# Four edits at the seams between the stages of a graph network stack

## The chip, the cores and the metric

The kernel runs on one core of a Trainium2 chip. A core has TensorE (PE, matrix products), VectorE (DVE), ScalarE (ACT), GpSimd (POOL) and SyncE (SP, which here issues every DMA). The metric is the device time of one execution in microseconds, smaller is better. Weight loads of TensorE are shown apart, as PEld.

## The reference

128 graphs of 128 nodes with 128 features go through four layers, each followed by a residual sum and a layer norm:

```python
x = _layernorm(x + _L0_gnn_ref(x, adj, ...))   # prelu(adj @ (x W) + bias)
x = _layernorm(x + _L1_gnn_ref(x, adj, ...))   # adj @ (x W) + bias
x = _layernorm(x + _L2_gnn_ref(x, adj, nodemask, ...))
x = _layernorm(x + _L3_gnn_ref(x, adj, ...))

# _L2_gnn_ref: five gated steps over the same adjacency
A = (adj != 0).astype(x.dtype)
h = x
for l in range(5):
    m = jnp.einsum('bnd,de->bne', h, weight[l])
    agg = jnp.einsum('bij,bid->bjd', A, m)
    h = _gru_cell(agg, h, w_ih, w_hh, b_ih, b_hh)
return h * mask[..., None]

# _L3_gnn_ref: five node groups (25, 9, 7, 6 and 6 of the first 25 nodes), two graph convolutions each
h = _graph_conv(x_g, adj_g, W1[g], b1[g])      # relu(norm_adj @ (x W1) + b1), 256 hidden features
out_g = _graph_conv(h, adj_g, W2[g], b2[g])
fused = fused.at[:, idx, :].add(norm_w[g] * out_g)
```

## The kernel before

The kernel has three stages, and each engine has one program that goes through them in order; engines meet only at semaphores.

**Stage A** computes the first two layers, four graphs in a step, 32 steps (`STEPS_A`). A step is spread over six pipeline slots (`has(0)` to `has(5)`, a lag of 0 to 5 behind the newest step), so each engine runs `step_a` 37 times; the last five are a tail in which fewer and fewer slots have work. The slot of lag 3 forms the products of the second layer from `X1` (PE L1269, the last products being those with `yT`), lag 5 is ScalarE writing the normed result `x2` (L774, four instructions), after GpSimd has made its shift and scale (`NM1`, L621 and L625). `run_a` takes a function that is to be called ahead of one step of the tail: ScalarE copies the first two items' `x2` into the high halves of `X_OF` ahead of step 32 (L781), and VectorE makes the low halves (L1074) and the 0/1 adjacencies `A16` (L1078) ahead of step 34. All of VectorE's normalization (L915 statistics, L919 aggregation, L926 the normed `X1`) is in the same program.

**Stage B** is the gated layer. An item is four graphs at one of the five gated steps; there are 4 streams, 8 rounds, 160 items. A slot of `slot_b` serves several items at different lags: an item's products are at lag 2, its ScalarE work at lags 2 and 3, its last VectorE work at lag 4. For one item TensorE does, in order: three passes for `R` from the turned state `HT_HI`/`HT_LO` (L1313, L1314, L1318), eight small products with `A16` (L1342, bank `P_B`), three passes for `Z` and three for `N`, then nine passes with `PT_HI` and `PT_LO`. ScalarE writes `PT_HI` (L792) and VectorE `PT_LO` (L1143) from `P_B`; ScalarE applies the sigmoids (L822 for R, L849 for Z) and the tanh (L799). State is turned by DMA transpositions which SP issues: L532 for a gated step above the first, L529 for the first gated step of a stream in a round (its source is `X_OF`), L548 for the result. SP also issues the adjacency loads `load_b` (L490), and after the item with number 20 (`TURN`, the last of round 0) the weights of stage C, `v1` and `v2`, in two DMAs (L497, L499). GpSimd waits for all of `x2` before stage B, then makes `HT` for the first gated steps (L659), the low halves (L635), and late in a stream the sums and masks `YB` (L651, L640, L667).

**Stage C** is the last layer on 16 graphs a step, eight steps (`step_c`), with the norm of all nodes beside it. The first one begins with `support(0)` on TensorE (L1307), which is issued in the last slot of stage B; ScalarE copies it out of PSUM as `SP_T` (L868), TensorE multiplies by `v1` (`hid`, L1386) into two hidden halves, ScalarE and VectorE apply the bias and the relu (L889, L1214), and `v2` follows (L1419). VectorE adds the groups (L1179, seven instructions) and TensorE turns the sums (L1398). On ScalarE the copy of `support(0)` stands behind the end of `slot_b`, whose last work is the high half of the last item's state (L816), and that waits for the state itself (`b_h`, VectorE L1124). Steps of stage C run the leftovers of stage B in `rest(k)`.

## Time and profile before

| | |
|---|---|
| time, median of 3 runs | 1030.77 us (1025.63 to 1034.74) |
| the profiled execution, its own time | 1028.89 us |
| its span | 1027.1 us |
| busy share of PE, DVE, ACT, POOL | 94%, 84%, 79%, 78% |
| mean granted clock of TensorE | 0.979 |
| chain of work that ended last | PE 74%, DVE 17%, issue 3%, POOL 2%, ACT 1%, DMA 1%, SPq 1% |

The busy shares tell which engine has least idle time over the whole, not what each stage waits for. The chain is followed back from the last instruction: its shares say who set the end. A granted clock of 1.00 is TensorE's 2.4 GHz, 0.50 is 1.2 GHz. The span is 1.8 us shorter than the execution's own time.

### The profile page before, as it was taken

What the parts mean: (1) busy time and instruction counts of PE and PEld (TensorE: products, weight loads), DVE (VectorE), ACT (ScalarE), POOL (GpSimd) and SP (SyncE); (2) the same over time, 40 slices, a digit from 0 to 9 for tenths busy, and PEclk for the clock granted to TensorE, in tenths of its full rate; (3) what the DMA queues carried; (4) which work ended last, traced back from release to release, by engine and by line L of the source; (5) the groups of instructions that cost most, each with busy time, mean ns of one, the idle gap of its engine ahead of it and who ended that gap; (6) DMA issues with size and microseconds to landing.
All of it is one profiled execution on the core that took longest, in us unless ns stands there. A gap on an engine that the chain in (4) does not pass through costs nothing.

```text
span 1027.1 us, 20028 instructions
## 1 busy us (share of the span) xinstructions
PE 965.6 (94%) x6010; PEld 588.2 (57%) x6010; DVE 862.6 (84%) x2447; ACT 808.3 (79%) x1387; POOL 796.7 (78%) x867
## 2 busy tenths in 40 slices
PE   4899999799989999999999999999999999987794
PEld 2799999445545555555554555554555455566683
DVE  6799999678778987898898899889889878868896
ACT  6588888577778898788888879888888877855784
POOL 4698999565577877888798788888878778887765
PEclk9999999699999999999999999999999999998997
DMA  5355332233474365346436434443643643412243
GB/s 131 99 124 132 104 106 80 52 62 72 74 153 83 62 113 87 70 82 99 80 60 124 83 63 103 87 79 65 113 82 61 118 79 74 73 33 81 67 117 96
DMA packets 294983, 90.48 MB, mean 88 GB/s; under 512 B 222291, under 2 KB 294764, under 8 KB 294892
## 3 DMA queue, kind: packets, MB, share of 16 engines
q1 hardware_dynamic: 294892, 89.39, 43.0%
q8 instruction: 42, 0.69, 0.3%
q14 instruction: 49, 0.40, 0.1%
HBM read 28.58 MB, written 8.81 MB: 36 GB/s over the span
## 4 chain that ended last, share of the span: by engine, by line
PE 74%; DVE 17%; issue 3%; POOL 2%; ACT 1%; DMA 1%; SPq 1%; DVEq 0%; POOLq 0%; ACTq 0%
PE psum L1313 20%; PE psum L1314 20%; PE psum L1318 20%; PE psum L1342 7%; DVE st L915 4%; PE psum L1419 3%; DVE x L926 3%; DVE mv L919 2%; PE psum L1386 2%; DVE ws L1062 2%; DVE ws L1052 1%; PE psum L1269 1%; DMA shared<-shared 1%; PE psum L1405 1%; DVE shared L1190 1%
## 5 line engine op out<-in xcount | busy, mean ns | idle before, releaser
L676 POOL TENSOR_TENSOR shared<-shared 128x512 f32<-128x512 f32 x160 | 203.2, 1270 | 45.4 <-ACT shared L849 44.4
L635 POOL TENSOR_TENSOR shared<-shared 128x512 f16<-128x512 f32 x128 | 148.1, 1157 | 68.2 <-ACT shared L810 68.2
L1313 PE MATMUL psum<-shared,wh_hi 128*128 128x512 f16 x480 | 183.0, 381 | 6.6 <-DMA shared<-shared 6.5
L1318 PE MATMUL psum<-shared,wh_hi 128*128 128x512 f16 x480 | 182.7, 381 | 0.0
L1314 PE MATMUL psum<-shared,wh_lo 128*128 128x512 f16 x480 | 182.7, 381 | 0.0
L1313 PE MATMUL psum<-shared,wx_hi 128*128 128x512 f16 x480 | 182.2, 380 | 0.0
L1314 PE MATMUL psum<-shared,wx_lo 128*128 128x512 f16 x480 | 182.1, 379 | 0.0
L1318 PE MATMUL psum<-shared,wx_hi 128*128 128x512 f16 x480 | 181.9, 379 | 0.0
L1117 DVE SCALAR_TENSOR_TENSOR shared<-psum,bhn,shared 128x512 f32<-128x512 f32 x160 | 120.1, 750 | 63.0 <-ACT shared L822 60.1
L849 ACT ACTIVATE shared<-psum,brz,unscale 128x512 f32<-128x512 f32 x160 | 124.0, 775 | 53.2 <-PE psum L1318 53.2
L1143 DVE SCALAR_TENSOR_TENSOR shared<-psum,shared 128x512 f16<-128x512 f32 x160 | 110.5, 691 | 38.2 <-ACT shared L792 38.0
L792 ACT ACTIVATE shared<-psum 128x512 f16<-128x512 f32 x160 | 95.5, 597 | 49.6 <-PE psum L1342 49.6
L822 ACT ACTIVATE shared<-psum,brz,unscale 128x512 f32<-128x512 f32 x160 | 124.4, 777 | 6.7 <-PE psum L1318 4.8
L799 ACT ACTIVATE psum<-shared,nbn,nunscale 128x512 f32<-128x512 f32 x160 | 124.3, 777 | 1.1 <-DVE shared L1131 1.1
L1110 DVE SCALAR_TENSOR_TENSOR psum<-shared,psum 128x512 f32<-128x512 f32 x160 | 110.3, 689 | 4.9 <-ACT psum L799 1.6
L1124 DVE SCALAR_TENSOR_TENSOR shared<-psum,shared 128x512 f32<-128x512 f32 x160 | 108.8, 680 | 0.1
L1131 DVE TENSOR_TENSOR shared<-psum,shared 128x512 f32<-128x512 f32 x160 | 108.8, 680 | 0.0
L1342 PEld LDWEIGHTS psum<-shared 128*128 128x128 f16 x1280 | 84.9, 98 | 38.8 <-DMA shared<-shared 2.3
L1342 PE MATMUL psum<-shared 128*128 128x128 f16 x1280 | 98.1, 220 | 0.0
L810 ACT ACTIVATE shared<-shared 128x512 f16<-128x512 f32 x128 | 80.6, 629 | 10.9 <-issue 2.2
L1318 PEld LDWEIGHTS psum<-shared,wx_hi 128*128 128x128 f16 x480 | 46.7, 97 | 65.0 <-DVE shared L1143 23.7
L1318 PEld LDWEIGHTS psum<-shared,wh_hi 128*128 128x128 f16 x480 | 47.1, 98 | 57.1 <-issue 0.8
(170 smaller groups left out, 1878.0 us busy)
## 6 DMA issues: line engine op xcount, KB each, us to landing
adj<-in_adj_dram SPq DMA_DIRECT2D x32, 256.0 KB, 3.0
x<-in_x_dram SPq DMA_DIRECT2D x32, 256.0 KB, 3.5
adjr<-in_adj_dram SPq DMA_DIRECT2D x32, 256.0 KB, 3.1
out_dram<-shared SPq DMA_DIRECT2D x8, 768.0 KB
shared<-shared SPq DMA_TRANSPOSE x192, 3.1
out_dram<-shared SPq DMA_DIRECT2D x32, 50.0 KB
v<-in_L_gnn_W_dram SPq DMA_DIRECT2D x2, 640.0 KB, 6.0
x3q<-x SPq DMA_DIRECT2D x16, 50.0 KB
```

The source lines that it names most:

```text
L635: nc.gpsimd.tensor_tensor(HT_LO[s % 2], HT[s][:, :], HT_HI[s % 2], ALU.subtract).then_inc(b_htl, 1)
L676: nc.gpsimd.tensor_tensor(ZH[s % 2][:, :], ZW[s % 2][:, :], HT[s][:, :], ALU.mult).then_inc(b_zh, 1)
L799: nc.scalar.activation(C_B, RT[s % 2][:, :], ACT.Tanh, bias=nbn[:, 0:1], scale=nunscale[:, 0:1])\
L822: nc.scalar.activation(RT[s % 2][:, :], R_B, ACT.Sigmoid, bias=brz[:, 0:1], scale=unscale[:, 0:1]).then_inc(b_r, 1)
L849: nc.scalar.activation(ZW[s % 2][:, :], Z_B, ACT.Sigmoid, bias=brz[:, 1:2], scale=unscale[:, 1:2]).then_inc(b_z, 1)
L1110: nc.vector.scalar_tensor_tensor(C_B, ZW[s % 2][:, :], 1.0, C_B, ALU.subtract, ALU.mult)\
L1117: nc.vector.scalar_tensor_tensor(RT[s % 2][:, :], N_B, bhn[:, 0:1], RT[s % 2][:, :], ALU.add, ALU.mult).then_inc(b_t1, 1)
L1143: nc.vector.scalar_tensor_tensor(PT_LO[s % 2][:, :], P_B, UP_P / UP_H, PT_HI[s % 2][:, :], ALU.mult, ALU.subtract).then_inc(b_pl, 1)
L1313: mm(dst, w_h[:, col:col + P], h[:, :], start=start, stop=False)
L1314: mm(dst, w_l[:, col:col + P], h[:, :], start=False, stop=False)
L1318: return mm(dst, w_h[:, col:col + P], lo[:, :], start=False, stop=stop)
L1342: last = mm(cols(P_B, i), cols(half, i), cols(A16[s], i), start=h == 0 and i == 0, stop=h == 1 and i == G4 - 1, skip_group_check=True)
```

## The change

Four places are edited; no computation is added or left out.

1. **Transpositions.** SP issues the first two transpositions of stage B (L529, streams 0 and 1) right behind the two first adjacency loads, each as soon as the low half of its item is there (`b_sxl`), and no longer behind the third and the fourth adjacency load, which wait for `A16`. So that the low halves are there sooner, VectorE does its part for the first items (L1074, L1078) ahead of step 33 of stage A instead of step 34.
2. **The last x2.** ScalarE leaves out the last step of stage A's tail (four graphs of `x2`, L774) and does it in stage B behind the second item's Z sigmoid. GpSimd's wait for all of `x2` is taken out.
3. **Weights.** `v1` and `v2` are loaded in ten DMAs, each behind the transposition of one of the items 10 to 19 of round 0, instead of two behind item 20.
4. **The support.** ScalarE's copy of `support(0)` is issued ahead of the high halves (L816) of the last two items: the condition `gth(x) == GROUPS - 1` is that of stream 2 in the last round, the last item but one. The last item's high half is the one that waits for the state longest.

```diff
-        def run_a(eng, role, ahead_at=None, ahead=None):
+        def run_a(eng, role, ahead_at=None, ahead=None, leave=0):
...
-            for k in range(STEPS_A, total):
+            for k in range(STEPS_A, total - leave):
...
             for s in range(2):
                 load_b(s, 0)
-            def load_v():
-                sp.wait_ge(a_x2, STEPS_A)
-                sp.dma_start(v1[:, :].rearrange("p (g e) -> p g e", g=NG),
-                             l3_w1.rearrange("g p e -> p g e")).then_inc(w_ld_v, 16)
-                sp.dma_start(v2[:, :].rearrange("p (g c d) -> p g c d", g=NG, c=HC),
-                             l3_w2.rearrange("g (c p) d -> p g c d", p=P)).then_inc(w_ld_v, 16)
+
+            def blocks(t):
+                return t[:, :].rearrange("p (g c) -> p g c", c=P)
+            for s in range(2):
+                sp.wait_ge(b_sxl, s + 1)
+                sp.dma_start_transpose(blocks(HTP[s]), X_OF[s][:, :]).then_inc(b_tr[s], 16)
+
+            def load_v(i):
+                g = i // 2
+                if i == 0:
+                    sp.wait_ge(a_x2, STEPS_A)
+                if i % 2 == 0:
+                    sp.dma_start(v1[:, g * HC * P:(g + 1) * HC * P], l3_w1[g]).then_inc(w_ld_v, 16)
+                else:
+                    sp.dma_start(v2[:, g * HC * P:(g + 1) * HC * P].rearrange("p (c d) -> p c d", c=HC),
+                                 l3_w2[g].rearrange("(c p) d -> p c d", p=P)).then_inc(w_ld_v, 16)
...
-                    if l == 0:
+                    if l == 0 and nth(x) > 2:
                         sp.wait_ge(b_sxl, gth(x))
                         reach(sp, b_hn, nth(x) - 2)
                         reach(sp, b_h0, gth(x) - 2)
                         sp.dma_start_transpose(blocks(HTP[p]), X_OF[s][:, :]).then_inc(b_tr[p], 16)
-                    else:
+                    elif l > 0:
                         sp.wait_ge(b_htl, late(x))
                         sp.dma_start_transpose(blocks(HNP[p]), HTP[p][:, :]).then_inc(b_tr[p], 16)
-                if x and nth(x) == TURN:
-                    load_v()
+                if x and 0 <= nth(x) - TURN // 2 < 2 * NG:
+                    load_v(nth(x) - TURN // 2)
...
             run_a(pool, step_a)
 
-            pool.wait_ge(a_x2, STEPS_A)
             def slot_b(at):
...
-            run_a(act, step_a, STEPS_A, first_x)
+            run_a(act, step_a, STEPS_A, first_x, 1)
+
+            def support_out(k):
+                act.wait_ge(c_s, k + 1)
+                nc.scalar.activation(SP_T[:, :].rearrange("p (b x) -> p b x", b=2),
+                                     psum[:, 2 * 512:4 * 512].rearrange("p (b x) -> p b x", b=2)[:, :, 0:CS // 2],
+                                     ACT.Copy).then_inc(c_st, 1)
...
                 if x and x[0] == L - 1:
                     l, s, it = x
+                    if gth(x) == GROUPS - 1:
+                        support_out(0)
                     act.wait_ge(b_h, nth(x))
...
                     nc.scalar.activation(ZW[s % 2][:, :], Z_B, ACT.Sigmoid,
                                          bias=brz[:, 1:2], scale=unscale[:, 1:2]).then_inc(b_z, 1)
+                    if n == 2:
+                        step_a(STEPS_A + 4, (STEPS_A + 4) % 4, lambda lag: lag == 5)
...
-            run_a(dve, step_a, STEPS_A + 2, first_x)
+            run_a(dve, step_a, STEPS_A + 1, first_x)
...
-                    pe.wait_ge(w_ld_v, 16 * 2)
+                    pe.wait_ge(w_ld_v, 16 * 2 * NG)
```

## Rows read from the trace of the kernel before

**Rows 1.** Page, part 1: busy time, share of the span, instructions.
```profile
PE 965.6 (94%) x6010; PEld 588.2 (57%) x6010; DVE 862.6 (84%) x2447; ACT 808.3 (79%) x1387; POOL 796.7 (78%) x867
```

**Rows 2.** Waits of PE: who it waited for, us in total, times, longest.
```profile
PE psum L1419 <- DVE shared L1207: 8.7, 3, 5.1
PE psum L1313 <- DMA shared<-shared: 6.5, 2, 3.4
...
PE psum L1386 <- ACT shared L868: 3.9, 1, 3.9
```

**Rows 3.** Timeline, end of stage A: start, duration, instruction [idle before <- releaser].
```profile
187.61 1.11 DVE L926 TENSOR_SCALAR x<-ws,mv,rs 128x128 f32<-128x128 f32 x4 [0.16 <-POOL rs L607]
187.82 1.01 POOL L607 TENSOR_TENSOR rs<-ve,half 128x4 f32<-128x4 f32 x1
...
188.78 2.08 PE L1269 MATMUL psum<-adjT,x 128*128 128x128 f32 x8
...
190.86 1.26 DVE L1074 SCALAR_TENSOR_TENSOR shared<-x,shared 128x512 f16<-128x512 f32 x2
...
192.04 0.75 DVE L1078 TENSOR_SCALAR shared<-adjr 128x512 f16<-128x512 f32 x2
192.14 1.91 PE L1269 MATMUL psum<-w_sb,yT 128*128 128x128 f32 x8
...
193.45 16.25 SPq L529 DMA_TRANSPOSE shared<-shared  x4
...
197.47 0.61 PE L1313 MATMUL psum<-shared,wh_hi 128*128 128x512 f16 x1 [3.43 <-DMA shared<-shared]
...
198.34 1.65 ACT L774 ACTIVATE x<-ws,nm,rs 128x128 f32<-128x128 f32 x4 [3.11 <-POOL nm L625]
```

**Rows 4.** Busy by stretch; each engine's us and count, PEclk the granted clock.
```profile
186.00:202.00 16.00, 11.61 (x43) 8.19 (x44) 9.82 (x42) 9.14 (x21) 8.65 (x16) 0.50 0.29 67
...
203.00:209.00 6.00, 6.00 (x35) 2.93 (x34) 4.06 (x6) 4.13 (x7) 2.38 (x2) 1.00 0.23 44
```

**Rows 5.** Timeline, from the second item's Z sigmoid to the third item's low pass.
```profile
208.99 0.78 ACT L849 ACTIVATE shared<-psum,brz,unscale 128x512 f32<-128x512 f32 x1 [0.52 <-PE psum L1318]
...
210.08 0.60 ACT L792 ACTIVATE shared<-psum 128x512 f16<-128x512 f32 x1 [0.32 <-PE psum L1342]
...
211.55 0.10 PEld L1318 LDWEIGHTS psum<-shared,wx_hi 128*128 128x128 f16 x1 [0.27 <-DVE shared L1143]
```

**Rows 6.** Timeline of SP's issues, from round 0 to round 1.
```profile
278.46 2.57 SPq L532 DMA_TRANSPOSE shared<-shared  x1
...
283.39 3.99 SPq L529 DMA_TRANSPOSE shared<-shared  x1
...
293.41 1.23 SPq L529 DMA_TRANSPOSE shared<-shared  x1
...
297.74 1.23 SPq L529 DMA_TRANSPOSE shared<-shared  x1
```

**Rows 7.** Timeline of PE: first pass of the first item of round 1.
```profile
290.16 0.39 PE L1313 MATMUL psum<-shared,wh_hi 128*128 128x512 f16 x1 [3.07 <-DMA shared<-shared]
```

**Rows 8.** Page, part 6: issues of the weights; KB each, us from issue to landing.
```profile
v<-in_L_gnn_W_dram SPq DMA_DIRECT2D x2, 640.0 KB, 6.0
```

**Rows 9.** Timeline, from stage B to C and on: ACT, POOL, DVE.
```profile
901.76 0.61 ACT L816 ACTIVATE shared<-shared 128x512 f16<-128x512 f32 x1
...
903.98 0.86 ACT L868 ACTIVATE shared<-psum 128x848 f32<-128x848 f32 x1
...
922.38 2.04 POOL L651 TENSOR_TENSOR yb<-yb,maskT 128x512 f32<-128x512 f32 x2
...
925.59 5.18 DVE L1179 TENSOR_TENSOR shared<-shared 128x144 f32<-128x144 f32 x7
...
926.60 3.86 POOL L640 TENSOR_TENSOR yb<-yb,x 128x512 f32<-128x512 f32 x3
...
944.95 1.18 DVE L1179 TENSOR_TENSOR shared<-shared 128x144 f32<-128x144 f32 x7
```

More of the change, by code:

```diff
@@ L508, in load_c @@
                                  xv[:, :, t, :]).then_inc(c_ldx[k % 4], 16)
-            def blocks(t):
-                return t[:, :].rearrange("p (g c) -> p g c", c=P)
             def slot_b(at):
@@ L866, in step_c @@
                 if has(0):
-                    act.wait_ge(c_s, k + 1)
-                    nc.scalar.activation(SP_T[:, :].rearrange("p (b x) -> p b x", b=2),
-                                         psum[:, 2 * 512:4 * 512].rearrange("p (b x) -> p b x", b=2)[:, :, 0:CS // 2],
-                                         ACT.Copy).then_inc(c_st, 1)
+                    if k > 0:
+                        support_out(k)
                 if has(1):
```

## The prediction

> **What bounds the kernel now.** I read the page's busy shares first. TensorE is busy for 94% of the span [rows 1], so the edits can only bring in its idle time or time at the lower clock. Second the waits of PE, which tell what that idle time hangs on [rows 2]: 6.5 us on transpositions, in two waits, both ahead of an item's first pass (L1313), 3.9 us on ScalarE's copy of the support, and 8.7 us on VectorE inside stage C, which no edit names. Third the timeline around each of these places, to see what is late next when the wait goes. The granted clock by stretch [rows 4] shows one more loss at the first place: from 186 us to 202 us the clock was 0.50, that is 1.2 GHz, and from 203 us 1.00.
>
> The sum is made against the profiled execution, 1028.9 us, which is 1.9 us below the median of the three runs, 1030.8 us.
>
> **Seam A to B, what is won.** TensorE ends its last products of stage A at 192.14 + 1.91 = 194.05 us and starts stage B at 197.47 us, after 3.43 us of idle time that the transposition issued at 193.45 us ended: 4.02 us from issue to use [rows 3]. The two transpositions no longer stand behind the loads that wait for `A16`, and their sources come one tail step sooner. VectorE's four instructions for them (1.26 us for two L1074, 0.75 us for two L1078, 190.86 to 192.79, so 1.93 us) would start where L926 of step 33 starts now, at 187.6 us. The first low half is ready at about 188.2 us, and its transposition lands by 188.2 + 4.0 = 192.2 us. That is before TensorE is through with stage A, so the wait goes.
>
> But the same 1.93 us now stand ahead of L926, the `X1` for which TensorE's next product waits: that product started at 188.78 us, right behind L926 [rows 3]. It, the bias and `yT` products behind it, and so the end of stage A on TensorE move by 1.8 us (1.93 less the 0.16 that L926 waited anyway). Stage A then ends at 194.05 + 1.8 = 195.8 us and stage B starts there, not at 197.5: 1.6 us won, of the 3.4 that were idle. GpSimd has the last shift at 200.0 instead of 198.3 us, and no longer holds up anything with it.
>
> How much does the contended pair of engines add? L1074 ran beside GpSimd's work in the trace of before too, so I take its 1.26 us as measured. The Trainium skill (SBUF — State Buffer, Who interferes with whom) says that a VectorE instruction with two SBUF inputs, as L1074 is, contends with GpSimd's reads and that the second to issue is blocked till the first is done; moved, the second L1074 would start behind L607 at 187.82 us and be held to 188.83 us. By that rule the move costs about 0.7 us more and the win is 0.9 us, by the row alone 1.6 us.
>
> The clock: stage B ran 5.5 us at half clock (197.5 to about 203) before it rose. With the gap gone TensorE works on without the long stop. How long it stays low is not to be had from one trace; it lies between all of the 5.5 us, nothing won, and none of it, 5.5 / 2 = 2.7 us won. I take a third, 0.9 us, because the clock stayed low through the products of the tail as well: TensorE was busy for 11.6 of the 16 us from 186 to 202, at 0.50 throughout [rows 4].
>
> **Seam A to B, what is paid.** The last `x2` is 1.65 us of ScalarE [rows 3]. Before, it stood ahead of the first `PT_HI`, at the low clock. Now it stands between the second item's Z sigmoid, which ended at 208.99 + 0.78 = 209.77 us, and the third item's `PT_HI` at 210.08 us [rows 5]. There are 0.31 us free, so `PT_HI` is late by 1.65 - 0.31 = 1.34 us. Behind it on ScalarE stand the tanh and the R sigmoid; VectorE's `PT_LO` waits for it, and TensorE's low pass waits for that: its weight load already waited for L1143 for 0.27 us [rows 5], so there is no room. TensorE stops for 1.3 us in the third item and nothing gives that back, since it is what stage B goes by. Bounds: 0 us if other work shifts so that ScalarE has the room, 1.65 us if it has none. Sum of the seam: -1.6 - 0.9 + 1.3 = -1.2 us. Copies, adjacencies and `HT` for the first items are ready earlier than before against TensorE's need, and GpSimd's removed wait only released L659, whose result is not wanted until the Z sigmoid.
>
> **The weights.** At the change of round SP issued transposition L532 at 278.46 us, then two DMAs of 640 KB that took 6.0 us to land [rows 8], a load, and at 283.39 us the transposition for the next round's first item, whose issue alone took 3.99 us against 1.23 us of two later ones [rows 6]. TensorE waited for it 3.07 us, from 287.09 to 290.16 us [rows 7]. Without the weights this transposition can be issued by about 278.5 + 2.6 + 0.6 (the load) = 281.7 us and lands at 285.7 us, 1.4 us before its use. All 3.1 us are won. What do the ten pieces cost? Each is 128 KB behind a transposition; by proportion (6.0 us for up to 1280 KB) it occupies the queues for 0.6 us, or 1.2 us if 6.0 us is what one DMA of 640 KB took. Transpositions come 297.74 - 293.41 = 4.33 us apart and take some 4.0 us from issue to use at most, so a piece is off the queues when the next is issued. Cost 0 us; bounds 0 and 1 us each.
>
> **The support.** ScalarE's copy L868 now starts where L816 started, at about 901.8 us, and ends at 902.7 us instead of 904.84; TensorE starts L1386 2.1 us earlier. The two L816 behind it move by 0.9 and about 0 us: the last waits for the state anyway. Then VectorE and GpSimd decide. In the next step but one VectorE's seven adds (L1179) took 5.18 us, against 1.18 us for the same seven later, and they ran while GpSimd worked without a stop from 922.38 to 930.46 us [rows 9]: an add got through about once in each of GpSimd's instructions. GpSimd's own chain hangs on VectorE's statistics and on the last state, not on the copy, so it does not move. If the adds begin 2.1 us earlier, they meet three more of its instructions and end when these end, at 930.5 instead of 930.8 us. All that follows on VectorE, up to the wait of TensorE on L1207 [rows 2], moves by 0.3 us. Bounds: 0 us and the whole 2.1 us, if the seven keep their 5.18 us. I take 0.3.
>
> **Sum.** -1.2 - 3.1 - 0.3 = -4.6 us: 1028.9 becomes 1024.3 us against its own execution, and the median 1030.8 becomes 1026.2 us. I give 1026.
>
> **Rivals.**
>
> *The gains hold all through.* The clock rises with no delay (2.7 instead of 0.9 us), the moved `x2` finds room (0 instead of 1.3), the adds keep their length (2.1 instead of 0.3): 4.9 us more, 1021 us. For it speaks that the half clock and the stretched adds are both states of one execution; against it that three things must go together. The single ones give 1023 to 1025 us.
>
> *The first seam gives nothing.* The clock stays low as long as before, the early VectorE work is held by GpSimd, and the stop of the third item is the full 1.65 us: -0.9 + 1.65 = +0.7 us. The sum is then +0.7 - 3.1 - 0.3 = -2.7 us, 1028 us, which three runs can't tell from no change.
>
> *Slower: the pieces push the transpositions.* Before, one transposition behind the weights needed 3.99 - 1.23 = 2.8 us more to be issued. If each of the ten pieces does a share of that to the next one, each item of the second half of round 0 starts late. It is worth nothing as long as piece and transposition fit in the 4.33 us; from the point on at which a piece holds the queues beyond the next issue by more than the 0.3 us between 4.33 and 4.0, TensorE waits. At 1 us each that is +10 us, so 1026 + 10 = 1036 us. Against it: the loads of 256 KB stand ahead of transpositions in every round, and TensorE waited for a DMA only twice in all [rows 2].
>
> **How the numbers follow.** The forecast with its nearest variants (1023 to 1028 us) gets 0.62, the full gain 0.15, no gain at the first seam 0.15, slower 0.08. The runs of before spread over 9 us, so the time measured of an unchanged sum may be 4 us to either side; 1019 to 1032 us holds all but the slower case and a tail of the gains. About 1% is what a measurement of this kernel can tell from no change: 1020.5 and 1041.1 us. Faster by over 1% takes the full gain and a good run: 0.09. Slower by over 1% takes more than the pieces at 1 us: 0.03. Within 1%: 0.88.
>
> **What would show it.** In the profile after: the PE wait on DMA ahead of L1313 is gone in both places; stage B starts at 195.8 us, and L1074 stands ahead of the last L926, the last `X1` product near 190.6 us. The clock rises within 2 to 5 us of that start. L774 stands behind the second L849, followed by a PE wait on L792 or L1143 of 1.1 to 1.4 us. L868 stands ahead of two L816, the PE wait on it is 1.8 instead of 3.9 us; the first seven adds with GpSimd beside them take over 6 us, and the waits on L1207 grow. It would be wrong if L926 were not late (then the first seam wins 1.8 us more), if a PE wait on DMA showed up among items 10 to 19, or if stage C from 931 us on came 2 us earlier against its start.

## The result and the profile after

| | before | after |
|---|---|---|
| time, median of 10 runs | 1029.98 us (1025.63 to 1034.74) | 1022.38 us (1019.72 to 1027.32) |
| ratio, with its 95% interval | 1 | 0.9923 [0.9901, 0.9944] |
| profiled execution, span | 1028.9 us, 1027.1 us | 1027.3 us, 1025.5 us |
| mean granted clock of that execution | 0.979 | 0.975 |

The change makes the kernel 7.9 us faster by the ratio (5.8 to 10.2 us by its interval), 7.6 us by the medians; 4.6 us were forecast, less than the interval allows. One execution of all those made for this document, one of 1045.49 us of the kernel with unused products in the first steps, was in a slower state and is left out of its ratio. The profiled execution of after is the slowest of its ten runs. So its span says little, and the two traces have to be compared stage by stage. I cut them at four instructions that both kernels have: **t0**, the start of VectorE's last `ws<-un,nalpha,ws` of stage A (L1052 before, L1066 after); the start of stage B, which is its first matmul pass; the Z sigmoid of the 4th, 20th and 22nd item (L849, L863); and the start of stage C, the first product of `support(0)`. From here on line numbers are those of after: L1313 has become L1327, L1318 L1332, L1269 L1283, L926 L940, L1074 L1088, L1078 L1092, L774 L780, L792 L804, L1143 L1157, L868 L793, L816 L830, L1179 L1193, L1207 L1221, L607 L614, L640 L646 and L651 L657. In the kernels of the experiments the same lines have numbers that differ by up to 25.

| us | before | after | won |
|---|---|---|---|
| span's start to t0 | 182.56 | 188.09 | -5.53 |
| t0 to the start of stage B | 14.91 | 12.76 | 2.15 |
| start of stage B to the 4th Z | 20.18 | 19.49 | 0.69 |
| 4th Z to 20th Z | 69.48 | 69.34 | 0.14 |
| 20th Z to 22nd Z | 11.91 | 8.66 | 3.25 |
| 22nd Z to the start of stage C | 600.30 | 600.23 | 0.07 |
| start of stage C to the end | 127.76 | 126.93 | 0.83 |

From t0 on this one trace is 7.1 us shorter, which is within the interval of the timed runs. The set-up ahead of t0, which no edit touches, was 5.5 us longer in it. There the granted clock differed: one stretch of ten microseconds shows it. These are the windows of before and then of after (stretch, its length, busy us and instructions of PE, PEld, DVE, ACT, POOL, then the clock, the DMA share, GB/s):

```profile
30.00:40.00 10.00, 6.28 (x44) 5.33 (x45) 8.43 (x30) 5.10 (x10) 5.28 (x5) 1.00 0.37 106
```

```profile
30.00:40.00 10.00, 7.94 (x33) 6.75 (x33) 7.37 (x23) 3.96 (x7) 3.21 (x4) 0.50 0.18 52
```

In the same ten microseconds TensorE did 44 instructions at 2.4 GHz in the one and 33 at 1.2 GHz in the other, and was busier with fewer.

The waits of PE after (who it waited for, us in total, times, longest) answer to [rows 2]:

```profile
PE psum L1433 <- DVE shared L1221: 7.1, 3, 5.1
...
PE psum L1283 <- DVE x L940: 6.4, 9, 2.7
...
PE psum L1400 <- ACT shared L793: 1.7, 1, 1.7
...
PE psum L1327 <- ACT shared L804: 0.5, 1, 0.5
```

Both waits on a transposition (6.5 us) are gone. The wait on the support fell from 3.9 to 1.7 us. In their place stand one wait of 2.7 us on `X1` (L940) and 0.5 us on the `PT_HI` copy (L804). The waits on L1221 inside stage C fell from 8.7 to 7.1 us; those on the seven adds (L1193) rose from 5.2 to 6.0 us.

**The first seam**, timeline (start, duration, instruction), answers to [rows 3]:

```profile
192.90 1.26 DVE L1088 SCALAR_TENSOR_TENSOR shared<-x,shared 128x512 f16<-128x512 f32 x2
...
193.58 2.74 SPq L500 DMA_TRANSPOSE shared<-shared  x2
193.69 1.43 POOL L614 TENSOR_TENSOR rs<-ve,half 128x4 f32<-128x4 f32 x1
194.07 0.75 DVE L1092 TENSOR_SCALAR shared<-adjr 128x512 f16<-128x512 f32 x2
...
194.75 1.10 DVE L940 TENSOR_SCALAR x<-ws,mv,rs 128x128 f32<-128x128 f32 x4
...
195.90 1.97 PE L1283 MATMUL psum<-adjT,x 128*128 128x128 f32 x8 [2.73 <-DVE x L940]
...
199.15 1.91 PE L1283 MATMUL psum<-w_sb,yT 128*128 128x128 f32 x8
...
200.85 0.63 PE L1327 MATMUL psum<-shared,wh_hi 128*128 128x512 f16 x1
```

VectorE's work for the transpositions stands ahead of the last `X1`, TensorE waits 2.73 us for that, and then goes from its last product into stage B without a stop. The clock in three stretches behind it, answering to [rows 4]:

```profile
200.00:202.00 2.00, 2.00 (x8) 1.24 (x8) 0.80 (x2) 2.00 (x6) 0.00 (x0) 0.50 0.01 4
202.00:203.00 1.00, 1.00 (x10) 0.87 (x9) 0.90 (x6) 0.10 (x1) 0.00 (x0) 0.56 0.00 0
203.00:204.00 1.00, 1.00 (x7) 0.43 (x5) 1.00 (x7) 0.84 (x2) 0.60 (x2) 1.00 0.00 0
```

A mean of 0.56 from 202 to 203 us puts the rise at about 202.9 us, 2.0 us after the start of stage B. Before it came at the same 202.9 us, but there that was 5.4 us after the start.

**The third item**, timeline of the same stretch as [rows 5]:

```profile
210.71 0.78 ACT L863 ACTIVATE shared<-psum,brz,unscale 128x512 f32<-128x512 f32 x1 [0.52 <-PE psum L1332]
211.39 1.64 ACT L780 ACTIVATE x<-ws,nm,rs 128x128 f32<-128x128 f32 x4
...
212.93 0.58 ACT L804 ACTIVATE shared<-psum 128x512 f16<-128x512 f32 x1
...
213.56 0.39 PE L1327 MATMUL psum<-shared,wx_hi 128*128 128x512 f16 x1 [0.50 <-ACT shared L804]
...
214.28 0.10 PEld L1332 LDWEIGHTS psum<-shared,wx_hi 128*128 128x128 f16 x1 [0.61 <-DVE shared L1157]
```

ScalarE's 1.64 us of `x2` stand between the sigmoid and the copy, and TensorE stops twice for it. The third item took 5.30 us, 0.97 us more than the 4.33 us of its neighbours.

**The change of round**, SP's issues and TensorE's first pass, answers to [rows 6, 7]:

```profile
281.01 1.24 SPq L539 DMA_TRANSPOSE shared<-shared  x1
...
282.29 1.45 SPq L490 DMA_DIRECT2D adjr<-in_adj_dram  x1
283.85 1.24 SPq L536 DMA_TRANSPOSE shared<-shared  x1
...
289.47 0.38 PE L1327 MATMUL psum<-shared,wh_hi 128*128 128x512 f16 x1
```

The issue of the transposition is back at 1.24 us (3.99 us before) and the pass has no wait.

**From stage B to C**, answers to [rows 9]:

```profile
900.99 0.85 ACT L793 ACTIVATE shared<-psum 128x848 f32<-128x848 f32 x1
...
901.75 0.62 ACT L830 ACTIVATE shared<-shared 128x512 f16<-128x512 f32 x1
901.90 5.09 PE L1400 MATMUL psum<-shared,v 128*128 128x400 f32 x20 [1.72 <-ACT shared L793]
...
922.60 6.00 DVE L1193 TENSOR_TENSOR shared<-shared 128x144 f32<-128x144 f32 x7
...
926.07 3.70 POOL L646 TENSOR_TENSOR yb<-yb,x 128x512 f32<-128x512 f32 x3
...
928.53 0.86 DVE L1101 BATCH_NORM_STATS2 stb<-yb 128x6 f32<-128x128 f32 x4
```

The copy of the support (L793) is ahead of the high halves (L830) of the last two items. The seven adds (144, 96, four times 48 and 16 columns; the row has the form of the first) beside GpSimd grew from 5.18 to 6.00 us, and the statistics start at 928.53 us, while GpSimd is at work until 929.77 us.

### The profile page after: what moved, and what is told of

It reads as the page before. It is cut to its first block, busy times and chain, and to the rows that moved or that the text cites. A ratio compares the mean times of both kernels' runs of the same rounds, so it can differ in the third digit from the quotient of the medians.

```text
span 1025.5 us, 20035 instructions
## 1 busy us (share of the span) xinstructions
PE 970.8 (95%) x6010; PEld 594.0 (58%) x6010; DVE 862.2 (84%) x2447; ACT 808.3 (79%) x1387; POOL 796.1 (78%) x867
## 4 chain that ended last, share of the span: by engine, by line
PE 77%; DVE 17%; issue 2%; ACT 2%; POOL 0%; SPq 0%; DVEq 0%; DMA 0%; POOLq 0%; ACTq 0%
PE psum L1327 20%; PE psum L1332 20%; PE psum L1328 20%; PE psum L1356 7%; DVE st L929 4%; PE psum L1433 3%; DVE x L940 3%; PE psum L1283 2%; DVE mv L933 2%; DVE ws L1076 2%; PE psum L1400 1%; DVE ws L1066 1%; DVE shared L1204 1%; PE psum L1419 1%; DVE shared L1193 1%
## 5 line engine op out<-in xcount | busy, mean ns | idle before, releaser
L1327 PE MATMUL psum<-shared,wh_hi 128*128 128x512 f16 x480 | 182.5, 380 | 0.1
L1327 PE MATMUL psum<-shared,wx_hi 128*128 128x512 f16 x480 | 182.0, 379 | 0.5 <-ACT shared L804 0.5
L1332 PE MATMUL psum<-shared,wh_hi 128*128 128x512 f16 x480 | 182.2, 380 | 0.0
L1332 PE MATMUL psum<-shared,wx_hi 128*128 128x512 f16 x480 | 182.0, 379 | 0.1
L863 ACT ACTIVATE shared<-psum,brz,unscale 128x512 f32<-128x512 f32 x160 | 124.0, 775 | 53.3 <-PE psum L1332 53.3
L1157 DVE SCALAR_TENSOR_TENSOR shared<-psum,shared 128x512 f16<-128x512 f32 x160 | 110.6, 691 | 35.5 <-ACT shared L804 35.5
L804 ACT ACTIVATE shared<-psum 128x512 f16<-128x512 f32 x160 | 95.5, 597 | 46.8 <-PE psum L1356 46.8
L1332 PEld LDWEIGHTS psum<-shared,wx_hi 128*128 128x128 f16 x480 | 46.7, 97 | 65.2 <-DVE shared L1157 24.1
L1332 PEld LDWEIGHTS psum<-shared,wh_hi 128*128 128x128 f16 x480 | 47.0, 98 | 56.8 <-issue 0.3
```

What stands on the lines that cost most here:

```text
L863: nc.scalar.activation(ZW[s % 2][:, :], Z_B, ACT.Sigmoid, bias=brz[:, 1:2], scale=unscale[:, 1:2]).then_inc(b_z, 1)
L1157: nc.vector.scalar_tensor_tensor(PT_LO[s % 2][:, :], P_B, UP_P / UP_H, PT_HI[s % 2][:, :], ALU.mult, ALU.subtract).then_inc(b_pl, 1)
L1327: mm(dst, w_h[:, col:col + P], h[:, :], start=start, stop=False)
L1332: return mm(dst, w_h[:, col:col + P], lo[:, :], start=False, stop=stop)
```

## The experiments

The forecast is a sum over parts, so the first question is what each part is worth by itself; the second, why the first seam and the support gave more than their terms. My theory was at first the one on record. The rivals were that the parts depend on each other, that the clock's rise at the start of stage B is set by the stop ahead of it, and that VectorE's adds are bound by their own start and not by GpSimd's end.

### One part at a time

The weights alone are before with edit 3, the support alone before with edit 4, the first seam alone before with edits 1 and 2.

> The kernel before with the third edit alone: v1 and v2 in ten DMAs behind the transpositions of items 10 to 19. My theory: the one wait of TensorE at the change from round 0 to round 1 goes (3.07 us before, 3.3 us less from the last item's products to stage C in the profile after), and the pieces cost nothing: 3.1 to 3.3 us faster, no wait of L1313 on a DMA among the first 20 items but the one at the start of stage B. Rival, the pieces push transpositions: waits on DMA of 0.3 us and more among items 10 to 19, and less than 2 us won. Rival, the stall was only put off: a wait of 1 us or more on a DMA or on the adjacency in round 1, no gain.

> The kernel before with the fourth edit alone: the copy of support(0) ahead of the last two high halves. My theory of the prediction: TensorE starts its first products with v1 2.1 us earlier, but VectorE's seven adds two steps on are stretched beside GpSimd's sums and take it back: 0.3 us faster. From the profile after, where the statistics behind these adds came 1.4 us earlier against the start of stage C: 1.4 us faster. Rival, nothing takes it back: 2.1 us. Whatever the stretch of the adds, the clock in the two later waits for L1207 can add or take 1.5 us.

> The kernel before with the first two edits: transpositions ahead, VectorE's early work a step sooner, the last x2 behind the second item's Z sigmoid. By the prediction 1.2 us faster (1.6 for the start, 0.9 for the clock, 1.3 paid for x2). By the profile after, measured against the same product of stage A, 3.0 us faster: stage B starts 2.1 us earlier, the clock rises 2.1 us after its start and not 5.5, which is 1.7 us, and x2 costs 0.8 us. If the four edits add up, this run, only_weights and only_support together give the 7.6 us of the whole change.

| kernel | ratio to before | us | by the trace, t0 to the end |
|---|---|---|---|
| weights alone | 0.9970 [0.9955, 0.9985] | -3.1 | -4.1 |
| support alone | 0.9989 [0.9969, 1.0010] | -1.1 | -1.0 |
| first seam alone | 0.9961 [0.9946, 0.9976] | -4.0 | -3.7 |
| all of them | 0.9923 [0.9901, 0.9944] | -7.9 | -7.1 |

The three add up to -8.2 us beside the -7.9 us of all. Each interval is 1.5 to 2 us wide to either side, so no dependence of these three parts on each other is seen, and a small one is not excluded. (Edits 1 and 2, both in the first seam, do depend on each other: next experiment.) The weights are worth what [rows 7] says. The first seam was forecast at -1.2 us and is worth more. The support, forecast at -0.3 us, is not told from nothing by the timing alone, and rests on the experiments below.

A single trace of a stage is one execution, and its clock differs from the next one's. So the traces of all kernels that share a seam are set side by side. For the first seam (some of the kernels come in the experiments below; times in us from t0; the rise is counted from the start of stage B):

| traces | start of stage B | clock rises | 4th Z |
|---|---|---|---|
| seam of before: before, weights alone, support alone | 14.91, 15.51, 15.66 | 5.4, 3.7, 3.5 | 35.09, 34.84, 34.88 |
| seam of after: after, seam alone, products in the first steps, copy late, GpSimd light (early, late) | 12.76, 12.88, 12.88, 11.95, 11.95, 12.87 | 2.0, 0.5, 3.8, 0.7, 0.6, 2.9 | 32.25, 32.26, 33.22, 31.33, 31.33, 32.78 |

So the seam wins 1.6 to 3.8 us up to the 4th Z, 2.7 us in the mean of the two rows. How that divides between the start and the clock changes from one pair of traces to the next.

For the weights, the 20th to the 22nd Z took 11.91, 12.83, 11.24 and 13.54 us in the four traces with two DMAs and 8.66 us in all ten with ten DMAs. The stop is thus worth 2.6 to 4.9 us. In two of the four (support alone, and the next experiment) the granted clock was 0.50 for 3.4 us after TensorE's stop there, which adds to its price; in before it was not.

### The transpositions without the move of x2

```diff
-            run_a(act, step_a, STEPS_A, first_x, 1)
+            run_a(act, step_a, STEPS_A, first_x)
...
-                    if n == 2:
-                        step_a(STEPS_A + 4, (STEPS_A + 4) % 4, lambda lag: lag == 5)
```

This is the first seam alone, with the last `x2` where it was before (GpSimd's wait for it stays out).

> The first edit without the second: the last x2 stays in the tail of stage A, ahead of ScalarE's first PT_HI. Theory: stage B starts as early as with both, but the last shift comes from GpSimd only after the first products with A16, so x2 and behind it PT_HI are late, and TensorE waits for L792 or L1143 in the first item, by 2 to 3.5 us: 0 to 1.5 us faster than the kernel before, in all. Rival, x2 in the tail costs no more than in the second item's place (0.8 us): as fast as only_seam_ab, 3 us.

1034.25 us, ratio 1.0031 [1.0013, 1.0049]: slower than before by 3.2 us, where I expected 0 to 1.5 us of gain. The profiled execution is the slowest of the twelve, by its set-up (t0 at 190.30 us). Its trace from 209.2 us on:

```profile
209.20 0.61 ACT L843 ACTIVATE shared<-x 128x512 f16<-128x512 f32 x1
209.72 0.57 ACT L801 ACTIVATE shared<-psum 128x512 f16<-128x512 f32 x1
...
210.35 0.39 PE L1319 MATMUL psum<-shared,wx_hi 128*128 128x512 f16 x1 [3.73 <-ACT shared L801]
...
212.02 0.63 PE L1319 MATMUL psum<-shared,wx_hi 128*128 128x512 f16 x1
```

Stage B starts at t0 + 12.84 us, as early as in after. But ScalarE's last `x2` waits for GpSimd's last shift, which the longer tail made later (it starts at t0 + 17.35 us, against 15.78 us before), and the first `PT_HI` stands behind it in ScalarE's order. TensorE stops 3.73 us inside the first item and falls back to the lower clock: the passes, 0.39 us at 210.35 us, take 0.63 us from 212.02 us on. At the 4th Z it is 4.9 us behind the first seam alone (t0 + 37.17 against t0 + 32.26). So edit 1 is worth -4.0 us with edit 2 and +3.2 us without it. The 1.34 us that I booked as the price of the second edit buy about 7 us as timed, of which the traces show 4.9 us by the 4th Z. The sum never asked what `x2` would wait for if it stayed.

### VectorE's early part one step later

```diff
-            run_a(dve, step_a, STEPS_A + 1, first_x)
+            run_a(dve, step_a, STEPS_A + 2, first_x)
```

After, with VectorE's four instructions for the transpositions back behind L940, so that they delay nothing and the transpositions are late instead.

> The changed kernel, but with VectorE's early work for the first items (L1088, L1092) ahead of step 34 as before. What is won by the sooner step? Counted from VectorE's last L1066 of stage A: the first low half would be ready at 8.9 us, its transposition lands 4.0 us later, so stage B starts at 12.9 to 13.1 us, against 12.8 us in the profile after, where stage A's own end is late by the 1.9 us of early work. Theory: the two are worth the same at the start of stage B, but here TensorE stands still for about 1.5 us ahead of it, so the clock rises later: 0 to 1.5 us slower than the changed kernel, 6 to 7.5 us faster than the kernel before. Rival, the sooner step is what wins: 2 us and more slower than the changed kernel.

```profile
193.19 1.26 DVE L1088 SCALAR_TENSOR_TENSOR shared<-x,shared 128x512 f16<-128x512 f32 x2
...
193.87 2.73 SPq L500 DMA_TRANSPOSE shared<-shared  x2
...
197.24 0.39 PE L1327 MATMUL psum<-shared,wh_hi 128*128 128x512 f16 x1 [2.75 <-DMA shared<-shared]
```

TensorE waits 2.75 us for the DMA, and stage B still starts at t0 + 12.19 us, inside the 11.95 to 12.88 us of the traces with the seam of after. At the 4th Z it is 0.76 us behind after (33.01 against 32.25), but also inside the 31.33 to 33.22 us of those traces. Timed, the two are not told apart: 0.9936 [0.9910, 0.9962] beside 0.9923. So the win at the start of stage B comes from the transpositions no longer standing behind the adjacency loads; having their sources sooner adds nothing to it that these traces show. In this trace the clock rose 3.9 us after the start of stage B. But it rose 3.8 us and 2.9 us after it in two traces without a stop there, so that a stop ahead of the first f16 pass costs more than one ahead of the last fp32 products is not shown.

### The last x2 in four slots

```diff
-                    if n == 2:
-                        step_a(STEPS_A + 4, (STEPS_A + 4) % 4, lambda lag: lag == 5)
+                    if isinstance(n, int) and 2 <= n <= 5:
+                        if n == 2:
+                            wait_apart(act, a_nm1, STEPS_A)
+                        i = n - 2
...
```

(What is left out is the one ACTIVATE that makes `x2` of graph `i`.)

> The changed kernel with the last x2 spread: its four instructions of 0.41 us stand behind the Z sigmoids of items 2, 3, 4 and 5, one each, instead of all four behind item 2's. ScalarE has some 0.3 us free at that place of each item. Theory of the stall (PT_HI late by what goes beyond the free time, TensorE stops for it): the 0.97 us by which the third item is longer in the profile after shrink to at most 0.1 us for each of four items, so 0.5 to 0.9 us faster than the changed kernel. Rival, x2's stop is covered by something else behind it: no difference.

```profile
205.92 0.78 ACT L863 ACTIVATE shared<-psum,brz,unscale 128x512 f32<-128x512 f32 x1 [0.52 <-PE psum L1340]
206.60 0.48 ACT L869 ACTIVATE x<-ws,nm,rs 128x128 f32<-128x128 f32 x1
207.01 0.60 ACT L804 ACTIVATE shared<-psum 128x512 f16<-128x512 f32 x1
...
208.11 0.38 PE L1335 MATMUL psum<-shared,wx_hi 128*128 128x512 f16 x1
```

One graph takes 0.48 us of ScalarE, and the pass behind `PT_HI` has no wait. The third item takes 4.33 us like the others, so the whole 0.97 us is back, and nothing is paid in the items after it: the trace of the first seam alone has the same start of stage B (t0 + 12.88 us) and the same rise of the clock, and its 4th Z is at t0 + 32.26 us against 31.29 us here. That shows the price of edit 2 and how it is avoided. Timed 1021.40 us, 0.9916 [0.9883, 0.9949]: not told from after, whose interval is wider than a microsecond.

### Products that keep the clock up

```diff
+            def filler(n):
+                for _ in range(n):
+                    mm(bank[5][:, 0:GATE], wh_hi[:, 0:P], wx_hi[:, 0:GATE], start=True, stop=True)
...
+                    if tail:
+                        filler({0: 2, 1: 7, 2: 15}[k - STEPS_A])
...
+                    if tail:
+                        filler(4)
```

Matmuls whose result nobody reads stand where TensorE waits in the tail of stage A. In a second kernel three of them stand at each of two waits in the first five steps of stage A instead.

> The changed kernel, and TensorE does extra products of the same kind ahead of its waits in the tail of stage A (steps 32 to 36: 2, 7 and 15 ahead of the waits for X1, 4 ahead of those for yT), which cover most of its 0.7 to 2.7 us of idle time there. Theory: the clock then stays full through the tail, the last products take 1.2 and 1.5 us instead of 2.0 and 2.5, stage B starts 1.5 to 1.9 us earlier and the 2.1 us at half clock behind it go (1.0 us): 1.5 to 3 us faster than the changed kernel. Rival, the clock falls all the same: up to 1 us slower, by the extra products that a wait doesn't cover.

> The changed kernel, and TensorE does three extra products of 128x384 f16 into an unused bank ahead of each of two waits in the first five steps of stage A, so that it does not stand still in the set-up. Theory: what makes executions of one kernel spread over 9 us is the clock in the first 50 us. In the profile after it was at half from 30 to 46 us and stage A ended 5.5 us later than in the profile before, where it was full. With less idle time it stays full more often: median 1 to 4 us lower, and the spread narrower. Rival, the spread comes from elsewhere (stage C, the first loads): the spread stays and the extra products cost 0 to 2 us.

In the tail the clock stayed at 2.4 GHz, as it did in the last experiment below, which has the same products; in the twelve traces without them it was at 1.2 GHz for 3.4 to 17.1 us between t0 and the 4th Z. The products with the last `X1` took 1.16 us where they had taken 1.97 us:

```profile
193.51 1.16 PE L1283 MATMUL psum<-adjT,x 128*128 128x128 f32 x8 [0.30 <-DVE x L940]
...
196.57 0.38 PE L1340 MATMUL psum<-shared,wh_hi 128*128 128x512 f16 x1
...
197.47 1.65 ACT L780 ACTIVATE x<-ws,nm,rs 128x128 f32<-128x128 f32 x4 [0.64 <-POOL nm L632]
...
200.18 0.39 PE L1340 MATMUL psum<-shared,wx_hi 128*128 128x512 f16 x1 [1.05 <-ACT shared L804]
```

Stage B starts at t0 + 10.88 us, 1.9 us sooner than in after and 1.1 us sooner than in the earliest trace without fillers. But now TensorE is ahead of ScalarE, which is still at an `x2` when the first `PT_HI` could be copied, and 1.05 us go there. At the 4th Z 1.35 us are left (t0 + 30.90). Timed 1023.38 us, 0.9923 [0.9893, 0.9952]: no difference to after. With the fillers of the first steps the clock was up in the set-up, but so it was in three traces without them, with t0 at 182.56 to 183.29 us against 184.64 us here: the fillers cost 1.4 to 2.1 us. The time was 1025.09 us, 0.9939 [0.9917, 0.9961], where I had expected 1 to 4 us of gain on after; by the ratios it is 1.6 us slower, and the intervals do not tell the two apart. Nor is a narrower spread shown: its eleven runs lie within 5.0 us, and eight of the kernel with VectorE's part later, without fillers, within 4.2 us.

### The support: when the copy is made, with and without GpSimd

```diff
-                    if gth(x) == GROUPS - 1:
-                        support_out(0)
...
-                    if k > 0:
-                        support_out(k)
+                    support_out(k)
```

This is after without edit 4.

> The changed kernel with the copy of support(0) back at its old place. In the profiles so far the stretch from the first product of stage C to the end is 127.2 to 128.8 us with the late copy (four kernels) and 124.0 to 126.9 us with the early one (six). If the early copy is what does it: about 2 us slower than the changed kernel, 5.5 us faster than the kernel before, a stretch of 127 us and more, and VectorE's first seven adds start 1.4 to 2.1 us later against the start of stage C. By the prediction's 0.3 us: no difference that can be measured.

Two more kernels, one of after and one of this, take GpSimd's long instructions away from beside VectorE's adds: in the last round its sums (L646) work on one column of 512, and its masks (L657) on one of 128 for each graph.

```diff
-                    nc.gpsimd.tensor_tensor(YB[s][:, :], YB[s][:, :], of_group(x2, x), ALU.add).then_inc(b_y, 1)
+                    w = 1 if isinstance(it, int) and it == ROUNDS - 1 else G4 * D
+                    nc.gpsimd.tensor_tensor(YB[s][:, 0:w], YB[s][:, 0:w], of_group(x2, x)[:, 0:w], ALU.add).then_inc(b_y, 1)
...
```

> The changed kernel with GpSimd's late sums and masks of the last round cut to one column (L646, L657 for the last four items; these 16 graphs are not masked and summed in full), so that GpSimd does next to nothing beside VectorE's first seven adds. Theory: each add waits for one of GpSimd's instructions; without them the seven take 1.2 to 1.5 us and not 6.0, and what hangs on them comes over 4 us earlier. Rival, the adds are slow for their first use of the tiles or for the products beside them: still 5 us and more.

> The same cut in GpSimd's work as in light_early, and the copy of support(0) at its old place. If GpSimd's work is what takes back part of the early copy, the two light kernels differ by the whole of what the copy wins for TensorE, 2.1 us at the first adds, while the two full ones differ by less there (1.4 us in the profiles). Rival, the clock decides: the difference of the two light kernels is no larger than that of the full ones.

| | copy early (after) | copy late | early, GpSimd light | late, GpSimd light |
|---|---|---|---|---|
| us timed | 1022.38 | 1023.67 | 1017.32 | 1018.79 |
| ratio to before | 0.9923 | 0.9947 [0.9927, 0.9968] | 0.9892 [0.9869, 0.9916] | 0.9905 [0.9880, 0.9931] |
| start of C to the seven adds, us | 24.03 | 26.27 | 23.69 | 27.01 |
| the seven adds, us | 6.00 | 5.18 | 1.18 | 1.19 |
| start of C to the end, us | 126.93 | 127.04 | 119.29 | 121.90 |

The late copy, VectorE's timeline, and then the early copy with GpSimd light:

```profile
921.03 5.18 DVE L1190 TENSOR_TENSOR shared<-shared 128x144 f32<-128x144 f32 x7
...
926.13 0.86 DVE L1098 BATCH_NORM_STATS2 stb<-yb 128x6 f32<-128x128 f32 x4
```

```profile
915.61 0.47 POOL L647 TENSOR_TENSOR yb<-yb,x 128x1 f32<-128x1 f32 x3
...
916.50 1.18 DVE L1195 TENSOR_TENSOR shared<-shared 128x144 f32<-128x144 f32 x7
...
917.60 0.86 DVE L1103 BATCH_NORM_STATS2 stb<-yb 128x6 f32<-128x128 f32 x4
```

The same seven adds take 5.2 to 6.0 us beside GpSimd's long instructions and 1.2 us beside short ones: it is GpSimd that stretches them, and [rows 9] was read rightly in that. One of them by itself, in after:

```profile
926.07 1.25 POOL L646 TENSOR_TENSOR yb<-yb,x 128x512 f32<-128x512 f32 x1
926.10 1.30 DVE L1193 TENSOR_TENSOR shared<-shared 128x48 f32<-128x48 f32 x1
```

It ends 0.08 us behind the GpSimd instruction that it began with. So do five of the seven in after and four in before, within 0.05 to 0.16 us of an instruction's end; the others take 0.2 to 0.3 us.

The early copy lets the seven start 2.2 us sooner; they take 0.8 us longer, and the statistics behind them start 1.4 us sooner (start of C + 29.96 us against + 31.36 us in before). The seven full traces with the early copy have them at + 29.96 to + 29.99 us. Three of the five with the late copy have + 31.36 to + 31.37 us; the other two have + 32.06 and + 32.07 us, and in these the clock was at 1.2 GHz for 6.8 us, not 3.4 us, behind the start of stage C. With GpSimd light the two kernels differ by 3.3 us both where the adds start and where the statistics do, so there nothing is taken back. I had expected 2.1 us; the late one's clock was at 1.2 GHz for 6.8 us in the same place, the early one's not at all.

The light kernels leave work out, so their times tell the cost of the pair of engines only from above: 3.2 us (0.9892 against 0.9923) and 4.3 us (0.9905 against 0.9947), part of which may be GpSimd's own work.

Over stage C as a whole the five traces with the late copy took 127.0 to 128.8 us, 127.7 in the mean, and the seven with the early one 124.0 to 127.0 us, 125.9 in the mean: 1.8 us. Much of the spread inside a kind goes with the clock. The three traces with the late copy and 13.6 to 13.7 us at 1.2 GHz in the first 108 us of stage C took 127.2 to 127.8 us; the two with the early copy and 13.6 us at it took 125.2 and 125.6 us. After itself had 17.0 us at 1.2 GHz there and before 13.7 us, so that the 0.83 us between these two understates the edit. The timing alone (0.9923 against 0.9947, intervals overlapping) does not tell the two full kernels apart. In after TensorE's groups of twenty products behind waits on VectorE took

```profile
936.11 5.08 PE L1433 MATMUL psum<-shared,v 128*128 128x400 f32 x20 [1.80 <-DVE shared L1221]
...
954.39 6.44 PE L1433 MATMUL psum<-shared,v 128*128 128x400 f32 x20 [5.11 <-DVE shared L1221]
```

and in both light kernels the first of these two groups took 3.41 us, at the higher level, the second 5.60 and 4.88 us. Where the lower clock falls differs from one execution to the next.

### Both together

The fillers of the tail, and the last two groups of `x2` (not one) spread over the slots of items 1 to 8, one graph each.

```diff
-            run_a(act, step_a, STEPS_A, first_x, 1)
+            run_a(act, step_a, STEPS_A, first_x, 2)
...
+                    if isinstance(n, int) and 1 <= n <= 2 * G4:
+                        q, i = STEPS_A - 2 + (n - 1) // G4, (n - 1) % G4
...
```

(Left out are a wait for the shift of group `q` and the ACTIVATE of its graph `i`.)

> The changed kernel with the extra products in the tail of stage A (as warm_tail), and with the last two x2 left out of the tail and spread over items 1 to 8, one instruction behind each Z sigmoid. In warm_tail the first item's low pass waited for ScalarE, which was still at x2. Theory: that wait of 1 us shrinks by about 0.7 us, the third item's 0.97 us goes, and the 1.35 us won by the full clock stay: the fourth Z sigmoid stands 29.2 us behind the last L1066 instead of 32.25 us; about 3 us faster than the changed kernel, 10 to 11 us faster than the kernel before. Rival, ScalarE has no room in the first items, where it also makes the sources of items 3 and 4: less than 2 us.

The wait on ScalarE is gone, and another one is next, in the first item:

```profile
197.68 0.39 PE L1352 MATMUL psum<-shared,wx_hi 128*128 128x512 f16 x1 [0.82 <-DVE shared L1164]
```

The 4th Z is at t0 + 29.41 us, 2.84 us sooner than after and 1.9 us sooner than the earliest trace with the seam of after; stage C starts 1.9 us sooner than in after. Timed: 1020.06 us, 0.9914 [0.9893, 0.9936], where I had expected 10 to 11 us on before (it is 8.9 us). Its median is the lowest of the complete kernels, but its interval takes in that of after and that of the spread `x2`, so better than after is not shown. Not explained: in the traces single items far from every edit took 0.4 to 0.7 us longer (the 160th here, the 94th and the 61st in the other two kernels with fillers, the 57th in four kernels without). Whether the fillers' 0.9 us that is lost between the 4th Z and stage C is only this stays open.

## Why the prediction was right or wrong

The direction and the place of every part were right, and so was "within 1%". The forecast of 1026 us was 3.6 us high: the measured gain is 1.7 times the forecast one, and that the time still lies inside 1019 to 1032 us owes much to the 4 us that I added to either side. The rival that came nearer is the one in which the gains hold all through (1021 us), to which I gave 0.15; of its three conditions only parts came true. By the terms of the sum, with the one pair of traces of the table above:

| term | forecast | trace | |
|---|---|---|---|
| start of stage B | -1.6 | -2.15 | right mechanism, too small |
| clock behind it | -0.9 | -1.65 | too small |
| stop in the third item | +1.3 | +0.97 | right mechanism, too large |
| weights | -3.1 | -3.25 | right |
| support (to the statistics) | -0.3 | -1.39 | the step that failed |
| sum | -4.6 | -7.5 | -7.9 timed |

**Start of stage B.** The step was that VectorE's 1.93 us would push L940, and TensorE's end of stage A with it by 1.8 us. The last `X1` product was foretold near 190.6 us, t0 + 8.0, and came at t0 + 7.81; against before it moved by 1.59 us. From it to the start of stage B 4.95 us passed, where I had put the 5.27 us from that product to the end of the last one in before; these 0.3 us and the 0.2 us make the difference.

The win of 0.9 us, with the second L1088 held by GpSimd, did not come: the two took 1.26 us as before, with L1092 1.17 us behind the first's start. It was GpSimd that was held. Its L614 (193.69 us) began behind the second L1088, which had begun at 193.47 us, and took 1.43 us instead of 1.01 us; its L611 beside the first took 0.54 us instead of 0.20 us. (In before the same two had taken 1.33 and 0.55 us beside L1074.) The Trainium skill (SBUF — State Buffer, Who interferes with whom) says that whichever of the two engines issues first has the shared ports for its whole instruction and the other waits. The trace agrees with that here, with GpSimd as the loser, and in the seven adds of stage C, with VectorE as the loser. What was wrong is my order of issue: I took L614 to begin where it had begun in before, and did not see that the first L1088 would hold L611 and so push L614 behind the second.

**The clock.** I took a third of the 2.7 us that were to be had, by the argument that the clock had stayed low through the tail as well. In this pair it rose 2.0 us after the start instead of 5.4 us, worth 3.4 / 2 = 1.7 us. Over the traces of the table it rose 3.5 to 5.4 us after the start with the old seam and 0.5 to 3.8 us after it with the new one. Which of these an execution gets was not to be had from the one trace I had, and what sets it stays open: a stop ahead of the first pass isn't needed for a late rise, as two traces show. The start and the clock together were forecast at 2.5 us and measured at 3.8 us in this pair (3.7 us by the means, with the third item's 0.97 us added back). The guess was between two bounds with nothing to choose by; half would have been as good, and nearer.

**The third item.** ScalarE's L804 and VectorE's L1157 were named, and both waits came, 0.50 and 0.61 us (the latter that of the weight load). I counted 1.64 us less the 0.31 us that ScalarE had free; the item was longer by 0.97 us. The spread kernel gave exactly this back. What I did not see is that this edit is the condition of the first. I held the last `x2` to be merely ahead of `PT_HI` "at the low clock", where it waits for GpSimd's last shift and holds up the first item.

**The weights.** All steps came as told: 1.24 us for the issue, no wait, nothing among items 10 to 19, where the trace shows 0.14 us won and not a cost. The slower rival would have needed ten stops there; there is none. What the sum left out is the clock behind the stop at the change of round, which fell in two of four traces.

**The support.** TensorE started 2.2 us sooner against the start of stage C, and the adds met more of GpSimd's instructions and took 6.0 us: both foretold. What failed was "end when these end". The last add does not have to wait for GpSimd's last instruction to end: VectorE's seven adds were through at 928.60 us, GpSimd at 929.77 us, which against the start of stage C is where it had ended before (31.20 and 31.12 us). About one add for each instruction of GpSimd is a rate; starting 2.2 us sooner in the same sequence the adds were held by five of its instructions instead of four, and ended one instruction earlier, not at the same one. So 1.4 of the 2.2 us are kept (2.1 of 2.9 us against the two late traces with the longer low clock). TensorE's wait on the seven adds did grow, from 1.85 to 2.69 us; the one that I had named, on L1221, fell from 8.7 to 7.1 us in all, but 7.1 us stand in the trace of the weights alone too, with the late copy, so this fall is not the copy's alone. The prediction itself had named the sign of this error, stage C from 931 us on coming earlier against its start.

**The spread of the runs** went into the range as 4 us to either side. By the traces most of it is the clock of the set-up: t0 lay between 182.6 and 190.3 us in the traces of the kernels that do the same work there. With the granted clock at 0.50 for at most 3.4 us of the set-up (five traces) it lay at 182.6 to 183.3 us, for 6.8 to 6.9 us (six traces) at 185.0 to 185.7 us, for 17.1 us at 188.1 us and for 20.5 us at 190.3 us. A reader who compared the spans of the two profiled executions, 1027.1 and 1025.5 us, would have found 1.6 us and a wrong account.

## What to carry to other kernels

Before a move is costed, ask of every instruction that stays behind what it waits for now that its neighbours come sooner: an in-order engine's leftover (here 1.65 us of `x2`) turned 4.0 us of gain into 3.2 us of loss. Where two engines block each other, write down the order in which their instructions begin after the move, not before it. Work that is moved to a busy engine goes in pieces of the size of its free time; 0.48 us per item cost nothing where 1.65 us in one cost 0.97. Cut two traces at a common instruction behind the set-up before comparing them, since one execution's clock ahead of it was worth more than any part of this change.

## What the runs showed of the hardware

- TensorE's clock can be low while TensorE is busy: at 1.2 GHz from 30 to 40 us with 7.94 of 10 us busy on fp32 products in after, at 2.4 GHz with 6.28 busy in before. It rose 0.5 to 5.4 us after the f16 passes began in the nine traces of the first seam's table, up to 3.8 us after it without a stop ahead of them, and was at 0.50 again within 2 us of a stop of 3.73 us. Products that nobody reads kept it up through the tail in both kernels that had them, and were worth nothing that could be timed.
- Seven adds of 16 to 144 columns on VectorE took 1.18 us alone and 5.2 to 6.0 us beside GpSimd's 128x512 sums and masks, four or five of the seven ending with one of GpSimd's instructions; the statistics right behind them (0.86 us) were the same with GpSimd at work or not. The other way round, GpSimd's L614 took 1.43 us instead of 1.01 us when it began beside VectorE's L1088.
- An issue of a transposition behind two loads of 640 KB held SP for 3.99 us, and for 1.24 us when the same bytes went in ten pieces between the transpositions. The pieces cost nothing that the trace shows (4th to 20th Z 69.34 us, 69.48 us before).
